# Who makes the expert products: the bias addition on ScalarE for all outputs and the products on GpSimd, in two of four expert stages

## The chip, the cores and the metric

The kernel runs on one core of a Trainium2 chip. The metric is the device time of one execution in microseconds (us). The core's engines are TensorE (PE in the profile, PEld for its weight loads), VectorE (DVE), ScalarE (ACT), GpSimd (POOL) and SyncE (SP, which here only issues transfers).

## What is computed

One adaLN block on x of shape (4, 512, 128): a causal attention with 16 heads of 8, then a mixture of experts over slices of 16 channels (8 slices per token, 16 experts, the two best by a softmax of logits), each with a modulated layer norm ahead and a gated residual behind. All is float32. The part that the change touches is the experts' output:

```python
hmid = jax.nn.gelu(jnp.einsum('td,edi->tei', t, W1) + b1, approximate=False)
eo = jnp.einsum('tei,eio->teo', hmid, W2) + b2
sel = jnp.take_along_axis(eo, topi[:, :, None], axis=1)
comb = (sel * topw[:, :, None]).sum(axis=1)
...
out = comb.reshape(bs, L_, d)
return out @ Wo + bo
```

The kernel doesn't gather. It makes all experts' outputs, adds b2, and multiplies them by routing weights that are zero for the experts that weren't chosen.

## The kernel before

**Batches and stages.** The four batches b = 0 to 3 each have an attention part (its exponentials are called softmax in the code) and an expert stage. TensorE runs the softmax of batch b + 1 and then the expert stage of batch b. In the expert stages of b = 0 and 1 the row maxima of the scores of batch b + 2 are woven in ("with maxima"): the matmuls misc<-dense,block on TensorE and the TENSOR_REDUCE mx<-misc on VectorE (line 1028). The expert stage of b = 2 has instead the tail of batch 3's attention woven in, and that of b = 3 stands alone.

**An expert stage.** It has 16 outputs, n = 0 to 15, each a 128x512 tile, and goes in half-steps t = 0 to 17. Half-step t has, on TensorE:

- two hidden units (2t and 2t + 1, while t < 16): two bf16 matmuls each, w1s times tstack, into one of two pairs of banks of `big`;
- up to three units of maxima into the two banks of `misc`;
- output n = t - 2: eight fp32 matmuls of 32 columns of weights into `acc[:, n % 2]`.

ScalarE takes a hidden unit from `big` through Gelu into a ring of 8 (line 769, 128x1024). TensorE may fill a pair of `big` again when ScalarE has read it, so it can be two units ahead.

**The products.** The routing weights of output n come by a transfer from `wT` into `gm[:, n]` (SP issues 16 of them, one semaphore `w_spread[n]` for each). The product gm = (acc + b2) * gm is made in two ways:

- even n, and all n for b = 3: VectorE, one SCALAR_TENSOR_TENSOR (line 1148);
- odd n for b < 3 (`SHARED = NB - 1`): ScalarE adds the bias into one of two buffers, `osb` or `yT` (`add_bias`, line 809), and GpSimd multiplies (line 670).

ScalarE issues `add_bias(n)` behind the Gelu of unit 2t + 1 of half-step t = n + 2. It waits there for output n (`consumed`) and for GpSimd to have read the buffer (`wait_weighted(act, b, n - 4)`). TensorE waits before output n for the reading of output n - 2 (`wait_taken`). GpSimd (`experts_out`) issues behind each odd product two transfers of key blocks for batch b + 2 (line 446, 12 in all), and behind the products 7 and 9 two sums of halves each (`sum_halves`, line 682), which TensorE needs for `combine(here, 0, 0)` at t = 14. Products 14 and 15 are needed for the second `combine`, behind the last half-step.

**The shift.** Among the maxima stand two units "mT" for each batch. VectorE turns the transposed maxima into three bf16 parts: lines 1045 and 1046 (read misc), 1049 (CAST nm<-nmr, in SBUF alone), 1050 (TENSOR_TENSOR nm<-nmr,nm, two inputs in SBUF), and then goes on with line 1028. The first mT of a stage comes between the maxima behind output 9.

The order on each engine is the order of the code. Nothing is scheduled by a planner.

Of the kernel before, what the change touches and what calls it, by code (L numbers as in the profile page):

```python
# [82 lines left out]
TURN_AT, SUM_AT, ROUTE_AT = 16, 18, 20  # L83
EARLY = 4

SHARED = NB - 1

STEPS = [(2 * q + hp, half) for q in range(FH // 4) for half in range(2) for hp in range(2)]
EH = NEP // 2
# [138 lines left out]
def weighted(n):  # L228

    hp, half = STEPS[n // 2]  # L230
    return 2 * hp + n % 2, half
# [17 lines left out]
def build(nc, x, pack_a, pack_b, pack_c, w1_rows, shift_ones, out):  # L249
    with ExitStack() as ctx:  # L250
# [151 lines left out]
        def wait_consumed(eng, phase, c):  # L402

            eng.wait_ge(s["consumed"], phase[1] + c + 1)
# [43 lines left out]
        def wait_weighted(eng, b, n):  # L448

            eng.wait_ge(s[f"gm_ready{n % 2}"], b * (GMS // 2) + n // 2 + 1 + GMS // 2)  # L450

        def wait_taken(eng, b, n):

            if n % 2 and b + n // GMS < SHARED:
                eng.wait_ge(s["biased"], b * (GMS // 2) + n // 2 + 1 + GMS // 2)
            else:
                wait_weighted(eng, b, n)

# [116 lines left out]
        def _(pool):  # L575
# [54 lines left out]
            def k_blocks(b, blocks):  # L630
                for c, a, j in blocks:
                    block_diagonal(pool, k_block_of[b], c, a, j, 64, "k_block")
# [29 lines left out]
            def experts_out(b, blocks=(), between={}):  # L662


                blocks = list(blocks)
                for n in range(1, GMS, 2):
                    pool.wait_ge(w_spread[n], 16 * b + 32)
                    pool.wait_ge(s["gm_ready1"], b * (GMS // 2) + n // 2 + GMS // 2)
                    wait_taken(pool, b, n)
                    pool.tensor_tensor(gm[:, n, :], biased[n // 2 % 2], gm[:, n, :], ALU.mult).then_inc(s["gm_ready1"], 1)  # L670
                    k_blocks(b + 2, blocks[:2])
                    del blocks[:2]
                    if n in (7, 9):
                        sum_halves(b, range(n - 7, n - 5))
                    if n in between:
                        between[n]()
# [60 lines left out]
        def _(act):  # L737
# [66 lines left out]
            def add_bias(b, phase, n):  # L804

                _, half = weighted(n)
                wait_consumed(act, phase, n)
                wait_weighted(act, b, n - 4)
                act.activation(biased[n // 2 % 2], acc[:, 1, :], ACT.Identity,  # L809
                               bias=B["b2"][:, half:half + 1]).then_inc(s["biased"], 1)  # L810

            def experts(b, phase, between={}):
                for u in range(EXPERT):
                    if u in between:
                        between[u]()
                    src = big[:, 2 * (u % 2):2 * (u % 2) + 2, :]
                    dst = ring[:, u % RING, :].rearrange("p (k w) -> p k w", k=2)
                    if b == NB - 1 and u == EXPERT - 1:
                        for k in range(2):
                            transform("experts", phase, u, src[:, k], dst[:, k], ACT.Gelu, 1.0)  # L820
                    else:
                        transform("experts", phase, u, src, dst, ACT.Gelu, 1.0)

                    n = u // 2 - 2
                    if b < SHARED and u % 2 and n > 0 and n % 2:
                        add_bias(b, phase, n)
                if b < SHARED:
                    add_bias(b, phase, GMS - 1)

            def change_table(k, func):  # L830
                act.wait_ge(s["tabled"], k)
# [33 lines left out]
        def _(dve):  # L865
# [291 lines left out]
            def experts_out(here, phase, ahead=False, between={}, cb0_at=CB0_AT):  # L1157


                b = here[1]  # L1160
                for n in range(GMS):
                    if n % 2 == 0 or b >= SHARED:
                        _, half = weighted(n)
                        wait_consumed(dve, phase, n)
                        dve.wait_ge(w_spread[n], 16 * b + 32)
                        if here[0] == "last" and n == GMS - 1:
                            for _, cols, _ in ENDS:
                                product(n, half, cols).then_inc(s["gm_ready1"], 1)
                        else:
                            product(n, half, slice(0, T)).then_inc(s[f"gm_ready{n % 2}"], 1)  # L1170
                    if n + 2 == cb0_at:
                        comb(here, 0)
                    if ahead:
                        maxima(here, b + 2, CHUNKS[n + 2])
                    if n in between:
                        between[n]()
                if here[0] == "last":
                    dve.wait_ge(s["x1b_ready"], b + 1)
                    for part, cols, _ in ENDS:
                        comb(here, 1, part, cols)  # L1180
                    for part, cols, _ in ENDS:
                        sum_up(here, part, cols)
                    return
                comb(here, 1)
                if GMS in between:
                    between[GMS]()
                dve.wait_ge(s["x1b_ready"], b + 1)
                sum_up(here)
# [555 lines left out]
```

## Time and profile before

| | us |
|---|---|
| median of 3 runs | 404.51 (404.13 to 406.26) |
| the profiled execution | 403.76 |
| its span in the trace | 402.0 |
| PE busy | 339.3 (84%) |
| DVE busy | 290.0 (72%) |
| ACT busy | 256.4 (64%) |
| POOL busy | 132.9 (33%) |

The span is the time between the first and the last instruction in the trace; 1.76 us of the profiled execution lie around it. TensorE's granted clock is 0.975 over the span. Busy shares are means over all stages. The expert stage of b = 0 takes the stretch from about 136 to 187 us, that of b = 1 from about 226 to 276 us.

### The profile page before, as it was taken

How to read it: one execution, taken by the hardware profiler on the slowest of the kernel's cores; microseconds unless marked ns; L12 is line 12 of the kernel's file. 1: busy time of each engine (PE TensorE's matmuls, PEld its weight loads, DVE VectorE, ACT ScalarE, POOL GpSimd, SP SyncE). 2: the span in 40 equal slices, each digit the busy share in tenths (PEclk: the TensorE clock that was granted, in tenths of full speed). 3: DMA queues.
4: the chain of work that ended last, by engine and by line, in shares of the span. 5: the costliest groups of instructions: out<-in, count | busy, mean ns of one | idle time of the engine just before them, and what ended most of it. 6: DMA issues, size and time to landing. Idle time of an engine off the chain costs nothing.

```text
span 402.0 us, 7268 instructions
## 1 busy us (share of the span) xinstructions
PE 339.3 (84%) x2637; PEld 158.2 (39%) x2668; DVE 290.0 (72%) x590; ACT 256.4 (64%) x297; POOL 132.9 (33%) x175
## 2 busy tenths in 40 slices
PE   3758688888877899988987899898879898879996
PEld 3424254445543444434553534334444323222123
DVE  5879868898789877875789487874769445972343
ACT  8570443435159878865349878855437997968981
POOL 6345307201421324842313024941410035532500
PEclk9988699999899999999999999999989999999999
DMA  7334214100016055520026255520014355814552
GB/s 258 109 67 71 48 35 66 29 4 0 4 40 98 24 141 138 165 59 3 27 51 98 57 137 135 141 45 4 29 30 50 90 136 142 116 17 122 134 147 70
DMA packets 27115, 31.53 MB, mean 78 GB/s; under 512 B 6780, under 2 KB 17788, under 8 KB 27068
## 3 DMA queue, kind: packets, MB, share of 16 engines
q1 hardware_dynamic: 23372, 28.57, 31.2%
q0 software_dynamic: 3456, 2.39, 2.8%
q8 instruction: 21, 0.34, 0.4%
q10 hardware_dynamic: 252, 0.11, 0.2%
q14 instruction: 14, 0.11, 0.1%
HBM read 3.57 MB, written 1.05 MB: 11 GB/s over the span
## 4 chain that ended last, share of the span: by engine, by line
PE 51%; DVE 21%; issue 10%; ACT 9%; DMA 3%; POOL 2%; SPq 2%; DVEq 0%; ACTq 0%; POOLq 0%
PE misc L1290 17%; PE acc L1290 16%; PE big L1290 16%; DVE mx L1028 8%; ACT ring L769 6%; PE misc L1312 2%; DVE xn L972 2%; DMA block<-qk_turned 1%; DMA tstack<-tp 1%; ACT L802 1%; SPq L492 1%; SPq L517 1%; POOL block L446 1%; DVE stats L947 1%; POOL rpow L591 1%
## 5 line engine op out<-in xcount | busy, mean ns | idle before, releaser
L769 ACT ACTIVATE ring<-big 128x1024 f32<-128x1024 f32 (+2 forms) x225 | 198.2, 929 | 99.7 <-PE big L1290 98.4
L1028 DVE TENSOR_REDUCE mx<-misc 128x1 f32<-128x512 f32 (+7 forms) x155 | 87.8, 588 | 24.2 <-PE misc L1290 22.1
L1290 PE MATMUL acc<-ring,cb 128*32 128x512 f32 x512 | 67.8, 604 | 2.6 <-DVE gm L1148 1.5
L1290 PE MATMUL big<-dense,block 128*128 128x448 bf16 (+7 forms) x249 | 54.3, 318 | 7.4 <-ACT ring L769 7.1
L1290 PE MATMUL big<-tstack,w1s 128*128 128x512 bf16 x178 | 52.4, 381 | 5.6 <-ACT ring L769 3.9
L1290 PE MATMUL misc<-dense,block 128*128 128x320 bf16 (+7 forms) x167 | 42.0, 313 | 8.9 <-DVE mx L1028 8.6
L1148 DVE SCALAR_TENSOR_TENSOR gm<-acc,cb,gm 128x512 f32<-128x512 f32 (+1 forms) x41 | 30.0, 733 | 22.7 <-DMA gm<-wT 12.2
L1290 PEld LDWEIGHTS big<-dense,block 128*128 128x128 bf16 x256 | 30.8, 149 | 33.7 <-ACT ring L769 19.0
L446 POOL DMA_DIRECT2D block<-qk_turned x66 | 39.3, 601 | 7.9 <-DMA tstack<-tp 7.0
L670 POOL TENSOR_TENSOR gm<-osb,gm 128x512 f32<-128x512 f32 x12 | 15.8, 1316 | 76.4 <-ACT osb L809 76.4
L1290 PE MATMUL acc<-ring,vals 128*32 128x64 f32 (+7 forms) x512 | 40.7, 421 | 0.4
L1290 PEld LDWEIGHTS misc<-dense,block 128*128 128x128 bf16 x170 | 20.8, 149 | 48.5 <-DVE mx L1028 39.8
L1290 PE MATMUL big<-earlier_query,identb 128*128 128x64 bf16 (+2 forms) x176 | 36.7, 209 | 0.8 <-issue 0.6
L1290 PE MATMUL misc<-later_key,identb 128*128 128x64 bf16 (+2 forms) x155 | 32.2, 208 | 0.6 <-issue 0.4
L670 POOL TENSOR_TENSOR gm<-yT,gm 128x512 f32<-128x512 f32 x12 | 15.7, 1311 | 29.0 <-ACT yT L809 29.0
L777 ACT COPY qk_turned<-qk 128x512 bf16<-128x512 bf16 x12 | 12.3, 1088 | 20.0 <-DVE qk L987 15.8
L682 POOL TENSOR_TENSOR gm<-gm 128x512 f32<-128x512 f32 x16 | 20.7, 1297 | 11.1 <-DVE gm L1148 10.6
L1290 PEld LDWEIGHTS big<-tstack,w1s 128*128 128x128 bf16 x192 | 13.2, 98 | 27.3 <-ACT ring L769 19.0
L1290 PEld LDWEIGHTS big<-earlier_query,identb 128*128 128x128 bf16 x176 | 20.4, 116 | 0.9 <-issue 0.9
L609 POOL TENSOR_TENSOR marked<-minus_half 128x1 f32<-128x1 f32 x8 | 2.1, 257 | 53.0 <-ACT qk_turned L777 37.7
L1290 PEld LDWEIGHTS acc<-ring,cb 128*32 128x32 f32 x512 | 10.5, 108 | 22.8 <-issue 18.3
L1290 PE MATMUL misc<-tstack,gm 128*128 128x448 bf16 (+7 forms) x53 | 14.4, 323 | 5.0 <-DVE mx L1028 4.4
(163 smaller groups left out, 472.0 us busy)
## 6 DMA issues: line engine op xcount, KB each, us to landing
gm<-wT SPq DMA_DIRECT2D x64, 256.0 KB
dense<-qk SPq DMA_DIRECT2D x42, 64.0 KB
tstack<-tp SPq DMA_DIRECT2D x18, 128.0 KB, 4.3
block<-qk_turned POOLq DMA_DIRECT2D x66, 32.0 KB, 3.2
xs<-in_x SPq DMA_DIRECT2D x4, 256.0 KB, 8.1
ca<-in_pack_a SPq DMA_DIRECT2D x1, 769.0 KB, 7.3
out<-lg SPq DMA_DIRECT2D x3, 256.0 KB, 2.3
dense<-tp SPq DMA_DIRECT2D x6, 128.0 KB, 8.9
```

What stands on the lines that cost most here:

```text
L446: eng.dma_start(dst[r:r + NR, :, a, :], turned).then_inc(s[f"{stack}_stacked"], 16)
L492: sp.dma_start(dst[r:r + 2 * NR, :, :], qk[j][at:at + 64, :]).then_inc(s[done], 16)
L517: sp.dma_start(tstack_of[b][FD * c:FD * c + FD, :, :], tp[j][:, :]).then_inc(s["t_stacked"], 16)
L670: pool.tensor_tensor(gm[:, n, :], biased[n // 2 % 2], gm[:, n, :], ALU.mult).then_inc(s["gm_ready1"], 1)
L682: pool.tensor_tensor(gm[:, h, :], gm[:, h, :], gm[:, 4 + h, :], ALU.add).then_inc(s["summed"], 1)
L769: act.activation(dst, src, func, scale=scale).then_inc(s["ring_read"], 1)
L777: act.copy(qk_turned[j][:, :, :], qk[j][:, :].rearrange("r (s q) -> r q s", q=BLK)).then_inc(s["qk_turned"], 1)
L972: ins = dve.tensor_scalar(xn[:, t, :], src[:, t, :], mean[:, norm, t:t + 1], rstd[:, norm, t:t + 1], ALU.subtract, ALU.mult)
L1028: dve.tensor_reduce(mx[:, g, k:k + n, blk], src, AX.X, ALU.max).then_inc(s["misc_read"], 1)
L1148: return dve.scalar_tensor_tensor(out=gm[:, n, cols], in0=acc[:, n % 2, cols], scalar=B["b2"][:, half:half + 1], in1=gm[:, n, cols], op0=A ...
L1290: return pe.matmul(dst, lhsT, rhs, start=start, stop=stop)
L1312: ins = pe.transpose(bank(here, unit)[0:P, P * t:P * t + P], src, ident[:, :])
```

## The change

Which outputs are shared between ScalarE and GpSimd is now told by `shared(b)`: all 16 for b = 0 and 1, the odd ones for b = 2 as before, none for b = 3. GpSimd now issues one key block behind each product instead of two behind each odd one; the sums of halves stay behind the products 7 and 9. The two buffers alternate with every shared output, so ScalarE waits for the product of the shared output two places earlier, which in these stages is n - 2 where it was n - 4.

```diff
-SHARED = NB - 1
+def shared(b):
+
+    return range(0 if b < NB - 2 else 1 if b < NB - 1 else 2 * FH, 2 * FH, 1 if b < NB - 2 else 2)
+
+
+SHARED_BEFORE = [sum(len(shared(k)) for k in range(b)) for b in range(NB)]
...
         def wait_taken(eng, b, n):
 
-            if n % 2 and b + n // GMS < SHARED:
-                eng.wait_ge(s["biased"], b * (GMS // 2) + n // 2 + 1 + GMS // 2)
+            b, n = b + n // GMS, n % GMS
+            if b >= 0 and n in shared(b):
+                eng.wait_ge(s["biased"], SHARED_BEFORE[b] + shared(b).index(n) + 1 + CREDIT["biased"])
             else:
                 wait_weighted(eng, b, n)
...
-                for n in range(1, GMS, 2):
+                for k, n in enumerate(shared(b)):
+                    ready = s[f"gm_ready{n % 2}"]
                     pool.wait_ge(w_spread[n], 16 * b + 32)
-                    pool.wait_ge(s["gm_ready1"], b * (GMS // 2) + n // 2 + GMS // 2)
+                    pool.wait_ge(ready, b * (GMS // 2) + n // 2 + GMS // 2)
                     wait_taken(pool, b, n)
-                    pool.tensor_tensor(gm[:, n, :], biased[n // 2 % 2], gm[:, n, :], ALU.mult).then_inc(s["gm_ready1"], 1)
-                    k_blocks(b + 2, blocks[:2])
-                    del blocks[:2]
+                    pool.tensor_tensor(gm[:, n, :], biased[k % 2], gm[:, n, :], ALU.mult).then_inc(ready, 1)
+                    k_blocks(b + 2, blocks[:1])
+                    del blocks[:1]
                     if n in (7, 9):
                         sum_halves(b, range(n - 7, n - 5))
...
                 _, half = weighted(n)
+                k = shared(b).index(n)
                 wait_consumed(act, phase, n)
-                wait_weighted(act, b, n - 4)
-                act.activation(biased[n // 2 % 2], acc[:, 1, :], ACT.Identity,
+                if k > 1:
+                    wait_weighted(act, b, shared(b)[k - 2])
+                elif b:
+                    wait_weighted(act, b - 1, shared(b - 1)[k - 2])
+                act.activation(biased[k % 2], acc[:, n % 2, :], ACT.Identity,
                                bias=B["b2"][:, half:half + 1]).then_inc(s["biased"], 1)
...
-                    if b < SHARED and u % 2 and n > 0 and n % 2:
+                    if u % 2 and n in shared(b):
                         add_bias(b, phase, n)
-                if b < SHARED:
-                    add_bias(b, phase, GMS - 1)
+                for n in range(GMS - 2, GMS):
+                    if n in shared(b):
+                        add_bias(b, phase, n)
...
                 for n in range(GMS):
-                    if n % 2 == 0 or b >= SHARED:
+                    if n not in shared(b):
```

**How the order moves.** GpSimd's queue in the expert stage of b = 0, from the product 5 (before: L670 is a product, L446 a key block, L682 a sum), before:

```order
L670 TENSOR_TENSOR gm<-osb,gm 128x512
L446 DMA block<-qk_turned 4x8x512 x2
L670 TENSOR_TENSOR gm<-yT,gm 128x512
L446 DMA block<-qk_turned 4x8x512 x2
L682 TENSOR_TENSOR gm<-gm 128x512 x2
L670 TENSOR_TENSOR gm<-osb,gm 128x512
L446 DMA block<-qk_turned 4x8x512 x2
L682 TENSOR_TENSOR gm<-gm 128x512 x2
```

and with the change, from the product 6 (L677 product, L451 key block, L689 sum):

```order
L677 TENSOR_TENSOR gm<-osb,gm 128x512
L451 DMA block<-qk_turned 4x8x512
L677 TENSOR_TENSOR gm<-yT,gm 128x512
L451 DMA block<-qk_turned 4x8x512
L689 TENSOR_TENSOR gm<-gm 128x512 x2
L677 TENSOR_TENSOR gm<-osb,gm 128x512
L451 DMA block<-qk_turned 4x8x512
L677 TENSOR_TENSOR gm<-yT,gm 128x512
L451 DMA block<-qk_turned 4x8x512
L689 TENSOR_TENSOR gm<-gm 128x512 x2
```

The product 8 now stands between the first two sums and the product 9, and one key block instead of two stands ahead of each pair of sums.

VectorE's queue in the same stage around the first shift, before:

```order
L1148 SCALAR_TENSOR_TENSOR gm<-acc,cb,gm 128x512
L1028 TENSOR_REDUCE mx<-misc 128x1 x4
L1045 TENSOR_SCALAR nm<-misc 32x128
L1046 SCALAR_TENSOR_TENSOR nmr<-misc,nm 32x128
L1049 CAST nm<-nmr 32x128
L1050 TENSOR_TENSOR nm<-nmr,nm 32x128
L1028 TENSOR_REDUCE mx<-misc 128x1
L1148 SCALAR_TENSOR_TENSOR gm<-acc,cb,gm 128x512
```

and with the change (L1040 is the maxima's line, L1057 to L1062 the shift's):

```order
L1040 TENSOR_REDUCE mx<-misc 128x1 x6
L1057 TENSOR_SCALAR nm<-misc 32x128
L1058 SCALAR_TENSOR_TENSOR nmr<-misc,nm 32x128
L1061 CAST nm<-nmr 32x128
L1062 TENSOR_TENSOR nm<-nmr,nm 32x128
L1040 TENSOR_REDUCE mx<-misc 128x1 x7
```

The products between the maxima are gone, and nothing else moved.

## Rows read from the trace of the kernel before

**Rows 1.** The page: engine, busy us (share of the span) xinstructions.

```profile
PE 339.3 (84%) x2637; PEld 158.2 (39%) x2668; DVE 290.0 (72%) x590; ACT 256.4 (64%) x297; POOL 132.9 (33%) x175
```

**Rows 2.** Windows of both stages, Gelu 6 to bias 13: busy us, PEclk, DMA, GB/s.

```profile
143.40:181.00 37.60, 35.76 (x251) 14.60 (x253) 29.89 (x51) 29.68 (x33) 19.86 (x23) 1.00 0.48 124
232.70:270.50 37.80, 35.96 (x256) 14.63 (x257) 30.03 (x51) 29.71 (x33) 19.97 (x23) 1.00 0.48 116
```

**Rows 3.** Waits, 141 to 187 us: who for whom, total us, times, longest.

```profile
DVE mx L1028 <- PE misc L1290: 8.0, 16, 0.8
ACT ring L769 <- PE big L1290: 7.0, 8, 1.7
...
PE misc L1290 <- DVE mx L1028: 2.1, 3, 1.4
```

**Rows 4.** Timeline of PE: start, us, line, form, xcount [idle before <-releaser].

```profile
141.74 1.06 PE L1290 MATMUL acc<-ring,cb 128*32 128x512 f32 x8
...
144.20 1.06 PE L1290 MATMUL acc<-ring,cb 128*32 128x512 f32 x8
...
168.29 1.07 PE L1290 MATMUL acc<-ring,cb 128*32 128x512 f32 x8
...
172.17 0.38 PE L1290 MATMUL misc<-dense,block 128*128 128x384 bf16 x1 [1.35 <-DVE mx L1028]
```

**Rows 5.** Timeline of ACT.

```profile
143.38 1.94 ACT L769 ACTIVATE ring<-big 128x1024 f32<-128x1024 f32 x2 [1.32 <-PE big L1290]
145.33 0.69 ACT L809 ACTIVATE osb<-acc,cb 128x512 f32<-128x512 f32 x1
146.13 1.94 ACT L769 ACTIVATE ring<-big 128x1024 f32<-128x1024 f32 x2
...
154.05 1.94 ACT L769 ACTIVATE ring<-big 128x1024 f32<-128x1024 f32 x2 [0.65 <-PE big L1290]
155.88 0.69 ACT L809 ACTIVATE osb<-acc,cb 128x512 f32<-128x512 f32 x1
156.56 1.94 ACT L769 ACTIVATE ring<-big 128x1024 f32<-128x1024 f32 x2
...
170.20 1.94 ACT L769 ACTIVATE ring<-big 128x1024 f32<-128x1024 f32 x2 [0.62 <-PE big L1290]
```

**Rows 6.** Timeline of POOL from the product 7.

```profile
162.05 1.27 POOL L670 TENSOR_TENSOR gm<-yT,gm 128x512 f32<-128x512 f32 x1 [2.90 <-ACT yT L809]
...
167.72 1.27 POOL L670 TENSOR_TENSOR gm<-osb,gm 128x512 f32<-128x512 f32 x1 [0.61 <-ACT osb L809]
168.94 1.19 POOL L446 DMA_DIRECT2D block<-qk_turned  x2
170.15 2.62 POOL L682 TENSOR_TENSOR gm<-gm 128x512 f32<-128x512 f32 x2
```

**Rows 7.** Timeline of DVE around the first shift of b = 0, and line 1050 at b = 1.

```profile
169.03 0.21 DVE L1049 CAST nm<-nmr 32x128 bf16<-32x128 f32 x1
169.28 2.30 DVE L1050 TENSOR_TENSOR nm<-nmr,nm 32x128 bf16<-32x128 f32 x1
171.51 0.60 DVE L1028 TENSOR_REDUCE mx<-misc 128x1 f32<-128x448 f32 x1
...
258.64 2.31 DVE L1050 TENSOR_TENSOR nm<-nmr,nm 32x128 bf16<-32x128 f32 x1
```

**Rows 8.** Timelines, 111 us: a DVE operation in SBUF beside one of POOL.

```profile
111.08 1.31 POOL L642 TENSOR_TENSOR xb<-xs,bog 128x512 f32<-128x512 f32 x1
...
111.25 1.16 DVE L969 SCALAR_TENSOR_TENSOR rstd<-rtmp,rpow 128x4 f32<-128x4 f32 x1
```

**Rows 9.** Timelines, 275 us: the second shift beside the product 15.

```profile
275.06 1.27 POOL L670 TENSOR_TENSOR gm<-yT,gm 128x512 f32<-128x512 f32 x1 [3.68 <-ACT yT L809]
...
276.17 0.24 DVE L1049 CAST nm<-nmr 32x128 bf16<-32x128 f32 x1
276.44 0.28 DVE L1050 TENSOR_TENSOR nm<-nmr,nm 32x128 bf16<-32x128 f32 x1
```

## The prediction

> **What bounds the kernel now.** I read the page first: TensorE is busy for 84% of the span, VectorE for 72%, ScalarE for 64% and GpSimd for 33% [rows 1]. Then the windows of the two stages that change. From Gelu 6 to the bias of output 13 TensorE is busy for 35.76 of 37.60 us at the full granted clock, VectorE and ScalarE for 29.9 and 29.7 us, GpSimd for 19.9 us [rows 2]. So TensorE sets the pace there, and the question is who makes it wait. The list of waits answers: VectorE waits for TensorE 16 times, ScalarE 8 times, and TensorE waits for VectorE 3 times, 2.1 us in all, one of them 1.35 us long [rows 3, 4]. None of these waits is for a product. The outputs 1 to 10 start at 144.20 and 168.29 us [rows 4]: 24.09 us for nine half-steps, 2.68 us each, all of it TensorE's own work.
>
> **VectorE loses 8 products in each stage.** That is 8 x 0.74 us = 5.9 us a stage, 11.8 us in all, of an engine that waits for TensorE before the maxima [rows 3]. Is there one product whose place on VectorE makes TensorE wait? The long wait of TensorE at 172.17 us is for the maximum that starts at 171.51 [rows 4, 7]. The order has the next product *behind* this maximum, and what delayed the maximum is the subtraction of line 1050, 2.30 us instead of the 0.28 that it takes in the second shift [rows 7, 9]. The two other waits are 0.75 us together [rows 3]. If both hung on a product, the gain would be 0.75 us a stage, 1.5 in all, and that is the far end. VectorE is idle for 7.7 of the 37.6 us, though, and waits there for TensorE [rows 2, 3], so I take 0.
>
> **ScalarE gets 8 more bias additions in each stage**, 0.69 us each, 5.5 us a stage. Free-running, a half-step of two Gelus and a bias takes 1.83 us from the first Gelu to the bias (154.05 to 155.88) and 0.68 to the next Gelu (156.56), 2.51 us [rows 5]. TensorE needs 2.68. The other end is the slowest spacing shown, 1.95 and 0.80 us, 2.75 in all (143.38, 145.33, 146.13) [rows 5], but those gaps are waits for TensorE. I take 2.51, since nothing was waited for in it. Does each new bias also fit where it stands? It can start when its output is done and must end before the next hidden unit. Output 10 is done at 168.29 + 1.07 = 169.36; with some 0.07 for the semaphore (output 1, done at 145.26, and its bias at 145.33) and 0.69 the bias ends at 170.12, and the next Gelu starts at 170.20, behind 0.62 us of idle time [rows 4, 5]. The new work fits into just this idle time, by less than 0.1 us; the idle time at 154.05 (0.65 us) is of the same kind. At output 0 it doesn't: 141.74 + 1.06 + 0.76 = 143.56 against 143.38, so Gelu 6 comes 0.18 us late. That costs nothing: Gelu 6 is then done at 144.58, and TensorE, which fills this pair of banks again behind output 1, gets there only after 144.20 + 1.06 = 145.26. The cover is thus at least 0.7 us deep. Cost 0; if the cover went at the 2.75 end, 13 x (2.75 - 2.68) = 0.9 us a stage would show.
>
> **GpSimd gets 8 more products in each stage**, 1.27 us each. A product with one key block takes 1.22 + 0.60 = 1.82 us [rows 6], under 2.68. The sums add 2.62 us behind the products 7 and 9. From the product 7, which stays at 162.05: key block to 163.87, sums to 166.5, product 8 from 166.6 to 167.86, key block, product 9 from 168.43 to 169.70, key block to 170.24, sums to 172.9, product 10 from 172.95 to 174.2, product 11 at 174.8, and from there on the products keep up with the biases. Who waits for this? The bias 12 needs product 10 and stands one half-step of 2.7 us behind bias 11, which needs output 11 (172.5 + 1.07): about 176.2, 2 us to spare. TensorE's `combine` needs the sums at t = 14, two to three half-steps behind output 11, which can't start before 172.17 [rows 4]: over 3 us to spare. The products 14 and 15 follow their outputs 2.6 us apart, as 15 did, so the stage's end stays. For the key blocks, still all issued by product 11, nothing changes. VectorE no longer waits for the transfer of `gm[:, 0]`, GpSimd does, with nothing behind it that is due. Cost 0.
>
> **The one wait that the change can move** is line 1050. Where a VectorE operation that reads two tiles in SBUF meets a GpSimd operation, it ends with the other: line 969 took 1.16 us instead of 0.16 and ended at 112.41, GpSimd's addition at 112.39 [rows 8]. Line 1050 ended at 171.58, GpSimd's first sum, which had started at 170.15, at about 171.43 [rows 6, 7]. It was held from 169.28 on, 0.87 us before that sum started, while GpSimd issued key blocks with the sum queued behind them. With the change the cast of line 1049, at 169.03, falls into product 9 (168.43 to 169.70). The cast at 276.17 fell into product 15, took 0.24 us and ended 0.08 us after it [rows 9], so I take it that a cast is held too. It would end at 169.78, line 1050 would be issued at 169.81, again behind a product, in front of a key block and a queued sum, and be held to that sum's end, 171.54 + 0.15 = 171.69 instead of 171.58. That is +0.11 us for TensorE in each stage, +0.22 in all. The other end: nothing holds it in the key block, it ends at 170.1, the maximum is done at 170.7, TensorE, free at 170.82 (172.17 - 1.35), doesn't wait, and each stage gains 1.35 us. I take the first, by the row at 169.28, the nearest to it.
>
> The Trainium skill ("SBUF — State Buffer", "Who interferes with whom") says that VectorE and GpSimd share a pair of ports under a lock that the first to start holds for the whole instruction, that a VectorE operation with two SBUF inputs contends only with a GpSimd operation that reads SBUF, and that casts can take the pair too; issuing descriptors should need only its write side, which the page calls inferred. By that rule line 1050, in the key block's time, would run at once: the other end, 401.6 to 401.8 us. The trace agrees for the line 969 and not for the one at 169.28, which was held before the sum started.
>
> **Sum.** The profiled execution, 403.76 us (span 402.0), + 0 (VectorE) + 0 (ScalarE) + 0 (GpSimd) + 0.22 = 403.98. The median of the runs is 0.75 above the profiled one: 404.7 us.
>
> **Rivals.**
> - *The hold goes.* Line 1050 gets through between product 9 and the sum. For it: the cast at 169.03 got through unheld 0.04 us after the product 9 had ended, with the sum already behind [rows 6, 7]; line 969 got through at once between two GpSimd operations [rows 8]. Against it: both times, 169.28 and 258.64, line 1050 was held before the sum had started [rows 7]. Gain 2 x 1.35 = 2.7: 401.8 us.
> - *ScalarE becomes the bound*, the one on the slower side. Place: the half-steps with even n, where the new bias fits by under 0.1 us. If each ends 0.3 us later than worked out (a longer semaphore path, a wait more in front of it) and the two units of cover are used up, ScalarE's half-step passes 2.68 and TensorE waits for `big`. Price up to the difference of 0.9 us worked out above, plus 0.3 for each of the 7 even outputs from 0 to 12, 2.1: some 1.2 to 3 us a stage, 2.4 to 6 in all, less what the 1.35 us stall gives ScalarE to catch up: about +2.8, 407.3 us. It decides from 0.17 us per half-step on. Against it: the 2.51 us.
> - *GpSimd is late at the first shift.* If product 8 or 9 slips by half a product, the cast and line 1050 are held that much longer, 0.6 us a stage: 405.9 us. From a slip of a whole product (1.28) on it is +2.6, 407.3 us.
> - *The change doesn't do what it says*: the order shows no product on VectorE between the maxima and 16 on GpSimd, so I give it nothing.
>
> **How the numbers follow.** Forecast 0.53, the hold goes 0.27 (with one of the two stages alone in it, 403.3), ScalarE bound 0.12, GpSimd late 0.08. The range leaves out less than the far end of the slow cases: 401.5 to 406.9 us. A measurement of this kernel can tell about 0.5% from no change, 2.0 us. Faster by more: most of the second case and little else, 0.26. Slower by more: ScalarE's case and a part of GpSimd's, 0.14. Within: 0.60.
>
> **What the profile would show.** Right: the outputs 1 to 10 still 24.1 us apart; ScalarE without its idle time before the Gelus of every second half-step; line 1049 at some 0.75 us, line 1050 near 1.9, and TensorE's wait of 1.4 us for the maximum behind it; VectorE's idle time up by some 12 us. Wrong: waits of TensorE big for ACT ring (ScalarE's case); line 1050 at 0.28 us and no wait at 172 (the hold goes); waits of the bias for POOL gm. The forecast fails if the hold of line 1050 follows another rule than the row at 169.28 suggests.

## The result: 1.3% slower

| | before | with the change |
|---|---|---|
| median of 4 runs each, us | 404.82 (404.13 to 406.26) | 409.88 (409.27 to 410.27) |
| the profiled execution, us | 403.76 | 410.11 |
| its span, us | 402.0 | 408.3 |
| granted clock of TensorE, mean | 0.975 | 0.962 |

The ratio is 1.0126, with a 95% interval of 1.0083 to 1.0169. I had forecast 404.7 us in a range of 401.5 to 406.9. A second measurement (e7, six runs, with 17 of the kernel before) gave 409.81 against 404.09 us, 1.0165 (1.0134 to 1.0196).

**What moved as it should.** The page of the changed kernel has VectorE's products down from 41 to 25 and GpSimd's up from 24 to 40. The first two of the lines that follow are line 670 before, the third is line 1148; behind the count stand the busy time, the mean ns of one, and the idle time ahead:

```profile
L677 POOL TENSOR_TENSOR gm<-osb,gm 128x512 f32<-128x512 f32 x20 | 26.0, 1298 | 67.2 <-ACT osb L820 66.8
...
L677 POOL TENSOR_TENSOR gm<-yT,gm 128x512 f32<-128x512 f32 x20 | 25.9, 1296 | 23.8 <-ACT yT L820 23.8
L1160 DVE SCALAR_TENSOR_TENSOR gm<-acc,cb,gm 128x512 f32<-128x512 f32 (+1 forms) x25 | 18.1, 728 | 22.4 <-PE acc L1302 12.8
```

The moved products took 11.9 us of work from VectorE (30.0 to 18.1), yet its busy time fell by 5.4 us only (290.0 to 284.6). Of the difference 2.9 us came back in the first shifts, as told below; the rest isn't traced.

**The outputs keep their pace up to the shift.** TensorE's timeline of the stage of b = 0, the outputs 1, 10 and 11, and the wait ahead of 11, which answers [rows 4]:

```profile
146.00 1.07 PE L1302 MATMUL acc<-ring,cb 128*32 128x512 f32 x8
...
170.11 1.06 PE L1302 MATMUL acc<-ring,cb 128*32 128x512 f32 x8
...
175.46 0.38 PE L1302 MATMUL misc<-dense,block 128*128 128x384 bf16 x1 [2.83 <-DVE mx L1040]
...
175.80 1.06 PE L1302 MATMUL acc<-ring,cb 128*32 128x512 f32 x8
```

Outputs 1 to 10 take 24.11 us, before 24.09. Then TensorE waits 2.83 us for a maximum, before 1.35.

**The cast is held through two GpSimd operations, the subtraction through a third.** VectorE's timeline at the first shift, the answer to [rows 7] (lines 1061 and 1062 are 1049 and 1050 of before), and GpSimd's beside it, to [rows 6]:

```profile
170.84 2.63 DVE L1061 CAST nm<-nmr 32x128 bf16<-32x128 f32 x1
173.51 1.36 DVE L1062 TENSOR_TENSOR nm<-nmr,nm 32x128 bf16<-32x128 f32 x1
174.79 1.67 DVE L1040 TENSOR_REDUCE mx<-misc 128x1 f32<-128x448 f32 x3
```

```profile
168.42 1.27 POOL L677 TENSOR_TENSOR gm<-osb,gm 128x512 f32<-128x512 f32 x1
169.63 0.60 POOL L451 DMA_DIRECT2D block<-qk_turned  x1
170.26 1.29 POOL L677 TENSOR_TENSOR gm<-yT,gm 128x512 f32<-128x512 f32 x1
171.48 0.60 POOL L451 DMA_DIRECT2D block<-qk_turned  x1
172.11 2.62 POOL L689 TENSOR_TENSOR gm<-gm 128x512 f32<-128x512 f32 x2
```

The product 9 (170.26) ends at 171.55. The cast, waiting since 170.84, doesn't get through there. It ends at 173.47, just behind the first sum (about 173.4). The subtraction, issued at 173.51, ends at 174.87, behind the second sum (174.73). Together they take 4.03 us from 170.84 on, before 2.55 us from 169.03 on: 1.48 us more, which is TensorE's longer wait (2.83 for 1.35).

**And the clock is lower behind such a wait.** The same place in the stage of b = 1, TensorE's timeline:

```profile
266.27 0.54 PE L1302 MATMUL misc<-dense,block 128*128 128x384 bf16 x1 [2.83 <-DVE mx L1040]
266.60 0.26 PE L1302 MATMUL misc<-later_key,identb 128*128 128x64 bf16 x1
266.80 1.94 PE L1302 MATMUL acc<-ring,cb 128*32 128x512 f32 x8
```

The eight matmuls of output 11 take 1.94 us instead of 1.06. Windows around it and around 129 us of the changed kernel (busy us of PE, PEld, DVE, ACT, POOL, then the granted clock, DMA share, GB/s):

```profile
128.00:134.00 6.00, 5.15 (x37) 2.58 (x38) 5.47 (x10) 4.11 (x7) 3.58 (x6) 0.72 0.27 63
262.00:266.00 4.00, 1.44 (x8) 0.57 (x8) 3.97 (x3) 2.73 (x4) 3.82 (x5) 1.00 0.27 72
266.00:270.00 4.00, 3.73 (x16) 1.09 (x18) 1.86 (x4) 0.73 (x2) 1.76 (x3) 0.57 0.07 14
```

A mean of 0.57 over 4 us is 3.4 us at the lower of the two levels (1.2 GHz), half the full 2.4 GHz, and the rest at the full one. Before, this place was at full clock [rows 2]. The stretch at 129 us lies *ahead* of the first changed instruction.

**Where the 6.3 us between the two profiled spans are.** The outputs 1 to 15 of a stage are a measure that leaves out what came earlier. Before they are 39.50 us apart (144.20 to 183.70) and 39.51 at b = 1; with the change 40.99 (146.00 to 186.99) and 42.46 (236.81 to 279.27). That is 1.49 + 2.95 us; the other 1.8 us had come by output 1 of b = 0 (146.00 for 144.20), 1.4 of them at the stretch at 129 us.

### The profile page after: what moved, and what is told of

Same layout as the page of the kernel before. It is cut to its first block, busy times and chain, and to the rows that moved or that the text cites. A ratio compares the mean times of both kernels' runs of the same rounds, so it can differ in the third digit from the quotient of the medians.

```text
span 408.3 us, 7298 instructions
## 1 busy us (share of the span) xinstructions
PE 342.3 (84%) x2637; PEld 158.3 (39%) x2668; DVE 284.6 (70%) x574; ACT 266.4 (65%) x313; POOL 152.9 (37%) x191
## 4 chain that ended last, share of the span: by engine, by line
PE 53%; DVE 22%; ACT 11%; issue 9%; DMA 2%; SPq 1%; POOL 1%; ACTq 0%; DVEq 0%; POOLq 0%
PE misc L1302 17%; PE acc L1302 17%; PE big L1302 17%; ACT ring L776 8%; DVE mx L1040 8%; DVE xn L984 2%; PE misc L1324 2%; DVE nm L1061 1%; DMA block<-qk_turned 1%; ACT L809 1%; ACT qk_turned L784 1%; SPq L498 1%; DVE stats L959 1%; DVE nm L1062 1%; POOL gm L677 1%
## 5 line engine op out<-in xcount | busy, mean ns | idle before, releaser
L1040 DVE TENSOR_REDUCE mx<-misc 128x1 f32<-128x512 f32 (+7 forms) x155 | 88.7, 589 | 33.3 <-PE misc L1302 30.8
L677 POOL TENSOR_TENSOR gm<-osb,gm 128x512 f32<-128x512 f32 x20 | 26.0, 1298 | 67.2 <-ACT osb L820 66.8
L451 POOL DMA_DIRECT2D block<-qk_turned x66 | 39.6, 604 | 8.1 <-DMA tstack<-tp 7.2
L677 POOL TENSOR_TENSOR gm<-yT,gm 128x512 f32<-128x512 f32 x20 | 25.9, 1296 | 23.8 <-ACT yT L820 23.8
L1160 DVE SCALAR_TENSOR_TENSOR gm<-acc,cb,gm 128x512 f32<-128x512 f32 (+1 forms) x25 | 18.1, 728 | 22.4 <-PE acc L1302 12.8
L689 POOL TENSOR_TENSOR gm<-gm 128x512 f32<-128x512 f32 x16 | 20.7, 1297 | 11.0 <-DVE gm L1160 10.4
L820 ACT ACTIVATE yT<-acc,cb 128x512 f32<-128x512 f32 x20 | 13.8, 690 | 12.3 <-PE acc L1302 12.3
```

Of the source, the lines that this page charges most:

```text
L451: eng.dma_start(dst[r:r + NR, :, a, :], turned).then_inc(s[f"{stack}_stacked"], 16)
L677: pool.tensor_tensor(gm[:, n, :], biased[k % 2], gm[:, n, :], ALU.mult).then_inc(ready, 1)
L689: pool.tensor_tensor(gm[:, h, :], gm[:, h, :], gm[:, 4 + h, :], ALU.add).then_inc(s["summed"], 1)
L820: act.activation(biased[k % 2], acc[:, n % 2, :], ACT.Identity, bias=B["b2"][:, half:half + 1]).then_inc(s["biased"], 1)
L1040: dve.tensor_reduce(mx[:, g, k:k + n, blk], src, AX.X, ALU.max).then_inc(s["misc_read"], 1)
L1160: return dve.scalar_tensor_tensor(out=gm[:, n, cols], in0=acc[:, n % 2, cols], scalar=B["b2"][:, half:half + 1], in1=gm[:, n, cols], op0=A ...
```

## The experiments

Theory **H**: GpSimd's operations hold VectorE's cast and subtraction in the first shift, and TensorE waits for that. Theory **A**: ScalarE's or GpSimd's additional work costs by itself. Theory **C**: the clock's lower stretches are the loss, and come by themselves. For each run the table has the ratio to the kernel before, timed beside it, and from the profile TensorE's longest wait for VectorE in the two stages and the distance of outputs 1 to 15. The waits of 0.4 us (e1, e2, e10, e12) stand later in the stage, ahead of output 15; at the first shift there is none as long there. The "low" marks a lower clock right behind the wait.

| run | median us (runs) | ratio (95%) | b = 0: wait, outputs 1 to 15 | b = 1 |
|---|---|---|---|---|
| before (profile of the case) | | | 1.35, 39.50 | 1.4, 39.51 |
| changed (case) | 409.88 (4) | 1.0126 (1.0083 to 1.0169) | 2.83, 40.99 | 2.83, 42.46 low |
| e7 changed again | 409.81 (6) | 1.0165 (1.0134 to 1.0196) | 2.84, 42.29 low | 2.8, 42.28 low |
| e3 b = 0 only | 407.57 (4) | 1.0113 (1.0069 to 1.0157) | 2.8, 42.43 low | 1.4, 39.52 |
| e4 b = 1 only | 406.40 (9) | 1.0075 (1.0037 to 1.0114) | 1.4, 39.50 | 2.84, 40.99 |
| e6 bias alone | 409.78 (4) | 1.0135 (1.0097 to 1.0172) | 2.45, 42.37 low | 2.45, 42.36 low |
| e8 changed, cast by reduction | 403.43 (10) | 0.9998 (0.9968 to 1.0029) | 1.51, 39.66 | 1.5, 39.66 |
| e2 changed, early sums | 403.45 (10) | 0.9998 (0.9964 to 1.0032) | 0.4, 38.49 | 0.4, 38.50 |
| e5, e11 changed, product waited for | 401.4 (1), 404.00 (12) | 0.9988 (0.9957 to 1.0018) | 0.6, 38.78 | 0.6, 38.78 |
| e10 changed, both cures | 403.28 (10) | 0.9988 (0.9961 to 1.0016) | 0.4, 38.24 | 0.4, 38.24 |
| e9 before, one key block | 401.47 (1) | | 0.78, 38.95 | 0.8, 38.95 |
| e1 before, early sums | 402.26 (10) | 0.9978 (0.9952 to 1.0005) | 0.4, 37.95 | 0.4, 37.93 |
| e12 before, both cures | 401.79 (10) | 0.9953 (0.9925 to 0.9981) | 0.4, 37.94 | 0.4, 37.93 |

**e3 and e4: each half of the change.** The choice of stages becomes a list; a stage that isn't in it keeps two key blocks behind each odd product.

```diff
-    return range(0 if b < NB - 2 else 1 if b < NB - 1 else 2 * FH, 2 * FH, 1 if b < NB - 2 else 2)
+    return range(0 if b in ALL_SHARED else 1 if b < NB - 1 else 2 * FH, 2 * FH, 1 if b in ALL_SHARED else 2)
```

> The change in the expert stage of b = 0 alone. Theory H: +1.5 us from TensorE's longer wait there (2.8 for 1.35), nothing in the stage of b = 1. Theory C: the stretch of lower clock at 129 us, which lies ahead of the first changed instruction of any stage, comes here too and adds 1.4 us (sum +2.9); if it hangs on the change itself it can't be there before the stage. Theory A: half of the loss, +2.5.

> The change in the expert stage of b = 1 alone. Theory H: +1.5 us at the first shift of b = 1 and nothing at b = 0; with the lower clock that followed this wait in the changed kernel (266 to 269 us) +1.4 more, 2.9 in all. If that lower clock belongs to the wait of 2.8 us, it must be here too; if it comes by the phase of the run, it may be missing. Theory A: half of the loss, +2.5, spread over the stage.

The loss goes with the changed stage and only with it: 2.8 and 1.4 us of wait in the one, 1.4 and 2.8 in the other. In the profiles it is 1.48 us without a lower clock (40.99 for 39.51, e4), as H says, and 2.93 with one (e3). The medians lie further off, 4.0 us above the kernel before for e3 and 2.8 for e4. e4's nine runs go from 404.20 to 408.58 us, and the profiled one, 404.92, is among the fast ones; where the others lost their time no profile shows. The stretch at 129 us, which C expected again in e3, was not in it. In e4 the lower clock behind the wait wasn't there in the profiled run: TensorE's output 11 at b = 1 took its ordinary time behind the same wait.

```profile
262.60 0.38 PE L1306 MATMUL misc<-dense,block 128*128 128x384 bf16 x1 [2.84 <-DVE mx L1044]
...
262.94 1.07 PE L1306 MATMUL acc<-ring,cb 128*32 128x512 f32 x8
```

**e1: take the sums away from the shift, in the kernel before.** Behind the products 5 and 7 in place of 7 and 9:

```diff
-                    if n in (7, 9):
-                        sum_halves(b, range(n - 7, n - 5))
+                    early = 2 if b < NB - 2 else 0
+                    if n in (7 - early, 9 - early):
+                        sum_halves(b, range(n - 7 + early, n - 5 + early))
```

> The kernel before, with the sums of halves of b = 0 and 1 behind the products 5 and 7 instead of 7 and 9. Theory H (a sum queued behind key blocks holds VectorE's cast and subtraction in the first shift): nothing is queued behind product 9 now, so line 1050 takes 0.28 us at both places, TensorE's waits of 1.35 us go, the span falls by 2 x 1.35 = 2.7 us (ratio to before about 0.993). Rival P (line 1050 was held for another reason than the sums, such as the key blocks' descriptors being issued): it stays at 2.3 us or is held to the end of the key blocks, 170.1, 0.9 us long.

GpSimd and VectorE at the first shift of e1:

```profile
167.33 1.27 POOL L670 TENSOR_TENSOR gm<-osb,gm 128x512 f32<-128x512 f32 x1 [0.62 <-ACT osb L810]
168.55 1.19 POOL L446 DMA_DIRECT2D block<-qk_turned  x2
172.54 1.27 POOL L670 TENSOR_TENSOR gm<-yT,gm 128x512 f32<-128x512 f32 x1 [2.80 <-ACT yT L810]
```

```profile
168.64 0.21 DVE L1050 CAST nm<-nmr 32x128 bf16<-32x128 f32 x1
168.88 0.28 DVE L1051 TENSOR_TENSOR nm<-nmr,nm 32x128 bf16<-32x128 f32 x1
```

The key blocks stand where they stood, and the subtraction takes 0.28 us. So the queued sum held it in the kernel before, and issuing key blocks doesn't. The stage is 1.55 us shorter, more than the 1.35 of the wait; all of it lies between output 10 and output 11, and what the rest of 0.2 us is isn't shown. The two stages together gain 3.1 us, the profiled span only 2.0 (402.0 to 400.0), and the ratio came out at 0.9978 where 0.993 was forecast. The profile shows a part of what is missing. In the softmax between the two stages it has a lower clock that the profile of the kernel before hasn't, behind the same waits for ScalarE (the windows are in order of before and e1):

```profile
216.00:222.00 6.00, 4.21 (x41) 2.62 (x42) 5.41 (x10) 5.22 (x9) 3.58 (x6) 1.00 0.27 64
```

```profile
216.00:222.00 6.00, 5.52 (x45) 2.83 (x48) 4.87 (x9) 3.80 (x6) 3.58 (x6) 0.72 0.22 58
```

The profiles of e10 and e12 have it at the same place.

**e9: move the first sum by half a microsecond, in the kernel before.**

```diff
-                    k_blocks(b + 2, blocks[:2])
-                    del blocks[:2]
+                    at_once = 1 if n == 9 and b < NB - 2 else 3 if n == 11 else 2
+                    k_blocks(b + 2, blocks[:at_once])
+                    del blocks[:at_once]
```

> The kernel before, with one key block instead of two between product 9 and its sums in b = 0 and 1 (three behind product 11). Theory H (the first queued sum holds line 1050 to the sum's end): the sum starts 0.6 us earlier and so does the release: line 1050 takes 1.7 us instead of 2.30 and TensorE's wait falls from 1.35 to 0.75 us in both stages. Rival P (a fixed penalty): 2.3 us stays.

```profile
167.79 0.21 DVE L1050 CAST nm<-nmr 32x128 bf16<-32x128 f32 x1
168.04 1.73 DVE L1051 TENSOR_TENSOR nm<-nmr,nm 32x128 bf16<-32x128 f32 x1
```

```profile
166.49 1.28 POOL L670 TENSOR_TENSOR gm<-osb,gm 128x512 f32<-128x512 f32 x1 [0.62 <-ACT osb L810]
167.71 0.60 POOL L446 DMA_DIRECT2D block<-qk_turned  x1
168.34 2.63 POOL L683 TENSOR_TENSOR gm<-gm 128x512 f32<-128x512 f32 x2
```

1.73 us and a wait of 0.78, as forecast: the release is the first sum's end (168.34 + 1.28 = 169.62, the subtraction ends at 169.77), wherever that stands.

**e2: the same cure for the changed kernel**, one sum behind each of the products 4 to 7.

```diff
-                    if n in (7, 9):
+                    if b < NB - 2 and n in range(4, 8):
+                        sum_halves(b, range(n - 4, n - 3))
+                    if b == NB - 2 and n in (7, 9):
                         sum_halves(b, range(n - 7, n - 5))
```

> The changed kernel with one sum behind each of the products 4 to 7 of b = 0 and 1. Theory H: the cast meets product 9 at most (under 1.1 us), the subtraction takes 0.28 us, TensorE's waits of 2.83 us go in both stages: 5.7 us less, and 404.3 us or less against 409.9. Theory C (most of the loss is the lower clock of three stretches of 3.4 us, which come by themselves): only the 2.96 us that the waits grew by go and the rest stays. Theory A (ScalarE or GpSimd with their 8 additional operations are what costs): nothing is gained, since GpSimd is loaded more at products 4 to 7.

VectorE, GpSimd and ScalarE's bias addition for output 10, each from its own timeline:

```profile
170.59 1.22 DVE L1063 CAST nm<-nmr 32x128 bf16<-32x128 f32 x1
171.84 0.28 DVE L1064 TENSOR_TENSOR nm<-nmr,nm 32x128 bf16<-32x128 f32 x1
```

```profile
170.42 1.29 POOL L677 TENSOR_TENSOR gm<-yT,gm 128x512 f32<-128x512 f32 x1
171.63 0.60 POOL L451 DMA_DIRECT2D block<-qk_turned  x1
172.26 1.29 POOL L677 TENSOR_TENSOR gm<-osb,gm 128x512 f32<-128x512 f32 x1
```

```profile
171.03 0.69 ACT L822 ACTIVATE osb<-acc,cb 128x512 f32<-128x512 f32 x1
```

The cast met product 9 and took 1.22 us, the subtraction 0.28, and TensorE waited 0.4 us at most. The time fell to that of the kernel before (0.9998), 6.4 us under the changed kernel, where C had only 2.96 us go. All the changed kernel's additional work is still there, so theory A falls as the cause of the loss, and C as the whole of it: this profile still has its stretch at 129 us.

**e8: take the cast out of the contention.**

```diff
-                link(dve.tensor_copy(nm[:, g, 1, :], nmr[:, :]))
+                link(dve.tensor_reduce(nm[:, g, 1, :], nmr[:, :].unsqueeze(2), AX.X, ALU.max))
```

> The changed kernel with the cast of the shift made by a reduction over an axis of one element (one input in SBUF, no faster mode). Theory H: the reduction isn't held beside product 9 (about 0.2 to 0.3 us), the subtraction then comes during product 9 and is held once, to the end of the first sum, instead of twice: TensorE's wait falls from 2.83 to about 1.5 us in both stages, 2.7 us less in all. Rival (any VectorE operation from SBUF to SBUF is held): the reduction takes 2.6 us as the cast did.

```profile
171.68 0.27 DVE L1061 TENSOR_REDUCE nm<-nmr 32x128 bf16<-32x128 f32 x1
171.99 2.40 DVE L1062 TENSOR_TENSOR nm<-nmr,nm 32x128 bf16<-32x128 f32 x1
```

```profile
171.12 1.28 POOL L677 TENSOR_TENSOR gm<-yT,gm 128x512 f32<-128x512 f32 x1
172.33 0.60 POOL L451 DMA_DIRECT2D block<-qk_turned  x1
172.96 2.61 POOL L689 TENSOR_TENSOR gm<-gm 128x512 f32<-128x512 f32 x2
```

The reduction runs in 0.27 us in the middle of product 9, and the subtraction is held once, to the first sum's end. The wait was 1.51 us, as forecast. The time gained more than the 2.7 us of the waits, 6.4 against e7: in its profile the clock stayed full in both stages. The distances account for 5.3 of the 6.4 us (42.29 and 42.28 to 39.66); where the rest came from is open. The Trainium skill ("SBUF — State Buffer", "Who interferes with whom") says that casts can contend with GpSimd, that operations with two SBUF inputs do so with a GpSimd operation that reads SBUF, and that reductions never do. The three lengths agree: 2.63 us for the cast in the changed kernel, 2.40 for the subtraction and 0.27 for the reduction here.

**e5 and e11: let GpSimd's queue stand at a wait when the product ends.**

```diff
+                    if b < NB - 2:
+                        wait_weighted(pool, b, n)
                     k_blocks(b + 2, blocks[:1])
```

> The changed kernel, where GpSimd's queue waits for the end of each product of b = 0 and 1 before it goes on to the key block and the sums. Theory H' (an operation already queued behind a key block takes the ports when the product ends; a waiting VectorE operation gets in only where GpSimd's queue stood at a wait): the cast now gets through at the end of product 9, 1.3 us earlier, some 0.8 us long, and the subtraction either runs at once (0.3 us) or is held to the end of the first sum (about 1.9 us). TensorE's wait of 2.83 us falls to about 1.5 or to 0. Rival P (GpSimd holds the ports through its key blocks as well): the cast stays at 2.63 us.

> The kernel of e5 timed: the cast is held once and the subtraction not at all. Profile of e5: TensorE waits 0.6 us at most. Expected about 1.7 us under the kernel before (its waits of 1.35 less what is left), ratio 0.995 to 0.996, and 8 us under the changed kernel, of which 4.5 are the waits and the rest the lower clock behind them.

```profile
169.00 0.60 POOL L451 DMA_DIRECT2D block<-qk_turned  x1 [0.30 <-POOL gm L677]
169.63 1.29 POOL L677 TENSOR_TENSOR gm<-yT,gm 128x512 f32<-128x512 f32 x1
171.21 0.60 POOL L451 DMA_DIRECT2D block<-qk_turned  x1 [0.30 <-POOL gm L677]
```

```profile
169.49 1.51 DVE L1063 CAST nm<-nmr 32x128 bf16<-32x128 f32 x1
171.04 0.28 DVE L1064 TENSOR_TENSOR nm<-nmr,nm 32x128 bf16<-32x128 f32 x1
```

The cast, issued at 169.49, *ahead* of product 9 (169.63) but with it queued, is held to its end (170.92), 1.51 us where some 0.8 was forecast, since it is held from ahead of the product. Then the queue stands at the wait, and the subtraction runs at once. So what holds is the operation that is queued behind, as e1 and e9 had it, and a wait in GpSimd's queue opens the gap.

The other runs fit this, and narrow it. In the code each sum has such a wait behind it (`summed`, in `sum_halves`), and at each sum's end the held operation got through, in the changed kernel twice. The product has none, and there the cast did not get through. But in e2 the cast did get through at product 9's end, at 171.81, with product 10 queued across a key block, and so did the subtraction in e10. Product 10 multiplies what bias addition 10 writes, and that ended at 171.72, product 9 at 171.71; in both stages of both runs the two ends lie within 0.01 us of each other. So the queued product was itself still waiting when product 9 ended. What held in the changed kernel was a sum that had nothing left to wait for. This reading is drawn from timelines and code; no run varies it by itself.

The time of e11 missed its forecast of 0.995 to 0.996: 0.9988, with 0.9957 as the interval's end, though its two stages are 0.72 us shorter each, as forecast. Of the 8 us under the changed kernel that were forecast, some 5.8 came (404.00 against 409.8).

**e6: ScalarE's part alone.** GpSimd makes the odd products, with two key blocks behind each as before, and VectorE the even ones from the biased copy (the lines for the key blocks are left out):

```diff
+                    if n % 2 == 0:
+                        continue
...
+                    if n in shared(b) and n % 2 == 0:
+                        dve.wait_ge(w_spread[n], 16 * b + 32)
+                        wait_taken(dve, b, n)
+                        dve.tensor_tensor(gm[:, n, :], biased[n % 2], gm[:, n, :], ALU.mult).then_inc(s["gm_ready0"], 1)
                     if n not in shared(b):
```

> ScalarE's part of the change alone: it adds the bias to all 16 outputs of b = 0 and 1, GpSimd makes the odd products as before, VectorE makes the even ones from the biased copy (two inputs in SBUF). Theory A0 (ScalarE's additions fit): the outputs 1 to 10 stay 24.1 us apart. The shift stands as before (line 1050 held 2.3 us, 1.35 us of wait). The even products on VectorE can now meet a product of GpSimd and be held; the products 8 and 10 stand near the sums (up to 1.3 us each), so 0 to 1 us a stage is open from that. Theory A: over 24.1 us and waits of TensorE big for ACT.

The outputs 1 to 10 take 24.33 us (144.22 to 168.55), 0.24 more than before, and TensorE waits for ScalarE 0.3 us in the stage. So far the additions fit. I had taken the shift to stand as before, and that was wrong:

```profile
165.12 1.22 DVE L1179 TENSOR_TENSOR gm<-osb,gm 128x512 f32<-128x512 f32 x1
166.26 2.49 DVE L1042 TENSOR_REDUCE mx<-misc 128x1 f32<-128x512 f32 x4
168.66 0.28 DVE L1059 TENSOR_SCALAR nm<-misc 32x128 bf16<-32x128 f32 x1
168.97 0.28 DVE L1060 SCALAR_TENSOR_TENSOR nmr<-misc,nm 32x128 f32<-32x128 f32 x1
169.28 2.25 DVE L1063 CAST nm<-nmr 32x128 bf16<-32x128 f32 x1
```

VectorE's product 8 was held by a sum (1.22 us for some 0.7), the cast came 0.25 us later than before, and that was enough: at 169.03 it had got through, 0.04 us behind the product 9's end [rows 6, 7]; at 169.28, with GpSimd's queue as before, it was held to the first sum's end. So whether the cast runs or is held hangs on a quarter of a microsecond, and ScalarE's part alone cost as much as the whole change (1.0135), by the shift and the clock behind it.

**e7: the changed kernel once more.**

> The changed kernel once more, on the chip of the other runs of this call, for its granted clock. Theory H: +2.96 us against before from the waits alone, so a ratio of about 1.0075; what is above that goes with the clock. If the longer wait brings stretches of lower clock, its mean clock is under that of before by 0.004 for each; if the stretches come by the phase of the run, one profile has them at other places than 129 and 266 us.

The waits are the same, 2.8 us twice. This time a lower clock followed both, and none came at 129 us:

```profile
140.00:172.00 32.00, 30.87 (x238) 12.98 (x237) 22.21 (x36) 30.13 (x36) 22.36 (x24) 1.00 0.54 142
172.00:177.00 5.00, 3.24 (x14) 0.89 (x15) 3.01 (x5) 0.94 (x2) 2.84 (x3) 0.66 0.40 91
...
264.00:269.00 5.00, 3.10 (x14) 0.75 (x15) 3.01 (x5) 0.97 (x2) 2.98 (x3) 0.66 0.07 12
```

Outputs 1 to 15 take 42.29 and 42.28 us: 2.8 us more than before in each stage, 5.6 in all, of the 5.7 that the medians differ by. Of the 2.8, 1.5 are the wait (e4) and 1.3 the clock. Of the six runs' mean clocks four are 0.962 or 0.963, 0.008 under the 0.970 that most runs of the kernel before have, which is two stretches as forecast; the profiled run has 0.967, though its profile has both: the mean also counts the lower clock of other places.

**What the clock follows.** The profiles have eight stages in which TensorE waited 2.4 us or more (changed, e7 and e6 two each, e3 and e4 one each). In six of them a lower clock followed at once. They have 20 stages with a wait of 1.5 us or less there (before, e1, e2, e5, e8 to e12 two each, e3 and e4 one each), and in none of them did it. So at this place the clock's part goes with the wait's length; why two of the eight were spared stays open. It is no threshold for the whole kernel, though. In the softmax ahead of an expert stage TensorE waits 1.3 us for ScalarE and 0.5 us soon behind, in the kernel before as well, and a stretch of 3.4 us at the lower clock followed there in six of the 28 cases: at 129 us in three profiles (changed, e2, e8), at 217 us in three others (e1, e10, e12). These come with and without a loss in the stages. What decides about them the runs don't show.

**e10 and e12: both cures, with and without the change.**

> The changed kernel with both cures: the cast by a reduction and the sums one each behind the products 4 to 7. Theory H: the shift is held at most by product 9, under 1 us, TensorE doesn't wait for it: about 2.7 us under the kernel before, 401.4 us, ratio 0.993, and no stretch of lower clock in the two stages. If the 16 products on GpSimd cost anything else, it is slower than the kernel before with early sums.

> The kernel before with both cures: the cast by a reduction, the sums behind the products 5 and 7. Theory H: the same waits as with the early sums alone, none at the first shift, 2.7 us under before, ratio 0.993. It has the old share of the products, so against e10 it tells what the moved bias additions and products are worth when nothing is held: 0 by the argument that TensorE's own work sets the pace.

e12 is the one kernel whose interval lies below 1: 0.9953, 2.4 us under before, and some 8 under the 409.8 us of the changed kernel, which was timed on another chip. Its stages are 1.56 and 1.58 us shorter than before. e10's are 0.30 us longer than e12's in each stage, all of it between output 10 and 11 (2.94 for 2.64 us), where the subtraction still takes 0.97 us, for 0.28, beside product 9. Everywhere else in the stages their outputs stand equally far apart, so where nothing is held the change is worth 0 there; with the rest of the hold it costs 0.3. e10 was forecast at 0.993 and came at 0.9988. Its median is 1.5 us above e12's, more than the 0.6 us of the two stages; the mean clock of its ten runs is lower (0.966 for 0.968), and whether that is all of the other 0.9 us isn't shown.

## Why the prediction was wrong, step by step

- **What bounds the stages**: right. TensorE sets the pace, 24.11 us for the outputs 1 to 10 where 24.1 was said.
- **VectorE's products are worth 0**: right. The stages of e10 and e12 differ by nothing else than the half-step of the held subtraction. VectorE's idle time did rise by 11.7 us, where some 12 were forecast, but by luck: 6.3 of them are the longer span.
- **ScalarE's additions cost 0**: right. The page has no longer wait of TensorE for ScalarE in the stage, and bias addition 10 ends 0.04 us ahead of the next Gelu (171.97 and 172.01), where "less than 0.1" was worked out (the idle time ahead of the Gelus is gone but for 0.22 us once). The rival in which ScalarE becomes the bound, which had the slower side, did not come.
- **GpSimd's queue**: right to 0.03 us. Products 8 and 9 were worked out at 166.6 and 168.43; they started at 168.42 and 170.26, 1.80 us of which is the later start of the stage.
- **The hold**: here it failed, in the sentence "It would end at 169.78". I let the cast through at product 9's end because line 969 [rows 8] and the cast at 276.17 [rows 9] had ended with the operation beside them. Behind neither of those stood a queued operation across a key block. The row at 169.28, which I used for the subtraction one sentence later, was of just this kind, and should have been used for the cast too. Then the cast ends with the first sum and the subtraction meets the second. That sum ends at 172.9 in the prediction's own times and the subtraction some 0.14 us behind it, at 173.04 instead of 171.58: + 1.46 us in each stage for the + 0.11 that I took (measured + 1.48). The term of + 0.22 us in the sum was thus + 2.96. Line 1049 took 2.63 us and line 1050 1.36, where 0.75 and 1.9 were forecast.
- **The clock**: missing, a term put at nothing without a reason. Nothing in the prediction asked what a TensorE wait of nearly 3 us brings. With the waits right, the forecast would have been 404.5 + 2.9 = 407.4 us, already outside the range of 401.5 to 406.9. The other 2.5 us of the 409.9 are the size of two lower stretches: the profiled run has one behind a wait, 1.5 us, and the one at 129 us, 1.4, and e7's has two behind the waits.
- **The rivals**: "The hold goes" had the sign of the one wait wrong, and so had the end worked out for an operation that nothing holds in the key block's time, 401.6 to 401.8 us. "GpSimd is late" gave nearly the right size for the waits, 407.3 us, from the wrong cause: GpSimd was on time.

## What to carry to other kernels

When work moves to GpSimd, list every VectorE operation from SBUF to SBUF (casts, copies, two inputs) that falls beside it and that somebody waits for, and give each the end of the operation that is *queued* behind, across transfers that are issued between, if that operation has nothing left to wait for. Such a small operation can be taken out of the contention, by a reduction over one element for a cast, by moving GpSimd's bulk work away from it, or by a wait in GpSimd's queue. And where a wait of TensorE grows, look at the granted clock behind it: here waits of 2.4 to 2.8 us cost 1.3 to 1.5 us more in six of eight cases.

## What was not expected of the hardware

- A cast issued 0.04 us behind a GpSimd operation's end ran at once, and one 0.26 us behind it was held 2.0 us, with the same queue. An operation on GpSimd thus held VectorE up to 0.9 us before it started, queued behind transfers. When exactly it takes hold stays open: in e2 the subtraction, 0.13 us behind a product's end, ran freely although the next product started 0.4 us later. And a cast issued just behind product 9 ran with the same sum queued (e9, 0.02 us behind) that held a cast already waiting at product 9's end (changed kernel).
- A wait of TensorE of 2.4 to 2.8 us was followed by 3.4 us at the lower clock in 6 of 8 cases, at 1.3 to 1.5 us each where it can be told (changed, e7, e3).
- The kernel before itself ranged from 401.25 to 405.88 us in 28 of 29 runs, with mean granted clocks from 0.983 (401.3 and 402.0 us) to 0.962 (405.7 to 405.9). So of the differences of 0.5% between the cured kernels some is clock that no edit explains, and the profile's distances between outputs are the sharper measure.
